# GNN kernel: GpSimd clears 960 idle numbers ahead of each batch of eight gathers in the two sum passes

## The chip, the cores and the metric

The kernel runs on one core of a Trainium2 chip. A core has TensorE (PE, matrix products; PEld is its loading of weights), VectorE (DVE), ScalarE (ACT), GpSimd (POOL), SyncE (SP) and 16 DMA engines; each engine works through its own queue in order, and the queues meet at semaphores. A gather that picks rows of a table by an index is issued by POOL. The metric is the device time of one execution in microseconds (us), as the median of several runs.

## The reference

The program is four graph networks in a row on 6250 nodes and 100000 edges (`src`, `dst`), each added to x and normalized. The change touches the fourth, whose two graph convolutions sum messages over edges:

```python
def gcn_conv(x, src, dst, W, b, n):
    h = x @ W
    loop = jnp.arange(n, dtype=src.dtype)
    s = jnp.concatenate([src, loop])
    d = jnp.concatenate([dst, loop])
    deg = jax.ops.segment_sum(jnp.ones(s.shape, h.dtype), d, num_segments=n)
    dinv = jnp.where(deg > 0, jax.lax.rsqrt(jnp.maximum(deg, 1.0)), 0.0)
    norm = dinv[s] * dinv[d]
    msg = h[s] * norm[:, None]
    out = jax.ops.segment_sum(msg, d, num_segments=n)
    return out + b
...
x = gcn_conv(x, src, dst, W1, b1, n)          # 256 -> 128
x = jax.nn.relu(batch_norm(x, g1, be1))
feats.append(x)
x = gcn_conv(x, src, dst, W2, b2, n)          # 128 -> 64
x = jax.nn.relu(batch_norm(x, g2, be2))
feats.append(x)
return jax.nn.relu(jnp.concatenate(feats, axis=1) @ Wfc + bfc)
```

The factor `dinv` of the source is put into the table's rows ahead of a pass and that of the target is applied behind it, so that the passes themselves are plain sums of table rows.

## The kernel before

The edges are sorted once by target into 832 groups (`NSLOT`) of 128 edges, such that a group's targets lie in one window of 128 nodes. For each group `order.row` has the 128 table rows to fetch, `order.place` the place of each target in its window, and `order.window` the window's number. Eight groups are a batch; there are 104 batches (`NBT`).

Stages follow one another with a barrier of all engines between them: sorting and ranking, then a1e, a2e, be and te (attention passes over the same edges, with dense stages between), then g1l (dense), the sum pass g1e on rows of 128 numbers, g2l, the sum pass g2e on rows of 64 numbers, n2 and the last product. A sum pass is `sum_pass`, written out in full for all 104 batches, with one queue for each engine:

- POOL (L1459 to L1471) issues eight gathers a batch (L1466), each of 128 rows into `rows`, a ring of four batches, that is 32 gathers. From the fifth batch on there is, ahead of the first and the fifth gather of a batch, an `apart` (L59): a wait for `s_summed` in an instruction of its own, which also counts up `s_passed`. It asks that the product that read this place of the ring is done.
- ACT builds `onehot` for a batch: eight times `distance` = |lane - place| (L1492), then relu(1 - distance) over all eight (L1495). It has two buffers.
- PE multiplies `onehot` by `rows`, one product a group (L1482; each is two matmul records in the trace), into one of eight PSUM banks. It waits for `s_onehot`, for the landing of four gathers at a time (`s_rows`), and for the bank (`s_added`).
- DVE adds the bank to the window's sums in `acc` (L1510); the window's number comes from a register that is loaded for four batches at once (L888).

No engine but POOL works for the fetching, and SP has nothing in these passes. Y is a large buffer of all stages; from g1 on it is split in `T1` and `T2` (L2321), 6400 numbers a partition each. `T1` gets the first convolution's output in g2l, `T2` the second's in n2; in both sum passes nobody reads or writes `T2`. In te, whose queue on POOL the prediction also reads, POOL has in each batch one product of its own (L1019) among the gathers (L1031), with `apart` waits on DVE's L1239.

Of the kernel before, what the change touches and what calls it, by code (L numbers as in the profile page):

```python
# [39 lines left out]
def wait(eng, sem, count):  # L40

    if isinstance(count, int) and count <= 0:
        return
    eng.wait_ge(sem, count)
# [14 lines left out]
def apart(eng, sem, count, passed):  # L59

    wait(eng, sem, count)
    eng.sem_inc(passed, 1)
# [1370 lines left out]
                batches(dve, step, NBT + 2, windows)  # L1433


def sum_pass(nc, c, stage, order, table, width, acc):

    RING = 4  # L1440
    with ExitStack() as stack:
        m = Memory(nc, stack, stage)
        rows = m.sb("rows", [P, RING, 8, width])
        onehot = [m.sb(f"onehot{b}", [P, 8, P]) for b in range(2)]
        distance = m.sb("distance", [P, 8, P], F16)
        ps_u = [m.ps(f"ps_u{b}", [P, 512]) for b in range(8)]
        s_rows = [[m.sem(f"rows{r}_{h}") for h in range(2)] for r in range(RING)]
        s_onehot, s_summed, s_added, s_distance, s_passed = (m.sem(x) for x in ("onehot", "summed", "added", "distance", "passed"))

        def lives(t):  # L1450
            return not isinstance(t, int) or 0 <= t < NBT

        def batches(eng, step, last=NBT, windows=None):
            for t in range(last):
                if windows is not None and t % RING == 0:
                    windows.load(t)
                step(t, t % RING)

        with nc.Block() as block:  # L1459
            @block.gpsimd  # L1460
            def _(pool):
                def gather(t, r):
                    for k in range(8):
                        if k % 4 == 0 and (not isinstance(t, int) or t >= RING):
                            apart(pool, s_summed, t * 8 + (k + 4 - RING * 8), s_passed)
                        pool.indirect_dma_start(  # L1466
                            out=rows[:, r, k, :], out_offset=None, in_=table,
                            in_offset=bass.IndirectOffsetOnAxis(ap=order.row[:, t * 8 + k:t * 8 + k + 1], axis=0),
                        ).then_inc(s_rows[r][k // 4], 16)

                batches(pool, gather)  # L1471

            @block.tensor
            def _(pe):
                def step(t, r):
                    b = r % 2
                    pe.wait_ge(s_onehot, t + 1)
                    for k in range(8):
                        if k % 4 == 0:
                            pe.wait_ge(s_rows[r][k // 4], t * 16 + (64 - r * 16))  # L1480
                        wait(pe, s_added, t * 8 + (k - 7))
                        pe.matmul(ps_u[k][:, 0:width], onehot[b][:, k, :], rows[:, r, k, :], start=True, stop=True).then_inc(s_summed, 1)  # L1482

                batches(pe, step)

            @block.scalar
            def _(act):
                def mark(t, b):
                    if lives(t):
                        wait(act, s_onehot, t)  # L1490
                        for k in range(8):
                            act.activation(distance[:, k, :], c.lane[:, :], ACT.Abs, scale=-1.0, bias=order.place[:, t * 8 + k:t * 8 + k + 1]).then_inc(s_distance, 1)  # L1492
                        act.wait_ge(s_distance, t * 8 + 8)
                        wait(act, s_summed, t * 8 - 8)
                        act.activation(onehot[b][:, :, :], distance[:, :, :], ACT.Relu, scale=-1.0, bias=1.0).then_inc(s_onehot, 1)  # L1495

                for t in range(NBT):
                    mark(t, t % 2)

            @block.vector  # L1500
            def _(dve):
                windows = Windows(nc, order, mybir.EngineType.DVE, -8, RING)

                def step(t, r):
                    for k in range(8):
                        if lives(t - 1):
                            mine = acc[:, bass.ds(windows.at(r, k - 8) * width, width)]
                            dve.wait_ge(s_summed, t * 8 + (k - 7))
                            wait(dve, s_added, t * 8 + (k - 8))
                            dve.tensor_tensor(mine, mine, ps_u[k][:, 0:width], ALU.add).then_inc(s_added, 1)  # L1510

                batches(dve, step, NBT + 1, windows)
# [546 lines left out]
def gnn_kernel(nc, x, src, dst,  # L2059
# [4 lines left out]
    tables = {n: nc.dram_tensor(f"table_{n}", [NPAD, n], F32, kind="Internal").ap() for n in (264, 66, 258, 256, 512, 128, 64)}  # L2064

    with ExitStack() as stack:
        m = Memory(nc, stack, "all")
        c = Keep()
        constants(nc, m, c)

        order = Keep()
# [11 lines left out]
        acc = m.sb("acc", [P, NW * 264])  # L2083
# [109 lines left out]
        with ExitStack() as st:  # L2193
# [24 lines left out]
            def drain_a2(act, ps, w, tile):  # L2218
# [6 lines left out]
                table=tables[66], table_width=66, through=ACT.Relu))  # L2225
# [12 lines left out]
        with ExitStack() as st:  # L2238
# [23 lines left out]
            def drain_ab(act, ps, w, tile):  # L2262
# [5 lines left out]
                 for h, a in enumerate((b_a1, b_a2)) for k in range(2)], x3, prepare, after_prepare=with_bias, fold=fold_attention,  # L2268
# [3 lines left out]
                            table=tables[258], table_width=258))  # L2272
# [3 lines left out]
        with ExitStack() as st:  # L2276
# [31 lines left out]
            def drain_vt(dve, ps, w, tile):  # L2308
# [8 lines left out]
                table=tables[512], table_width=512))  # L2317
# [3 lines left out]
        T1, T2 = Y[:, 0:NPAD], Y[:, NPAD:2 * NPAD]  # L2321
        dinv_of = small[:, 1, :]

        with ExitStack() as st:
# [17 lines left out]
            def drain_v(dve, ps, w, tile):  # L2342
# [5 lines left out]
                        first=Step(sources=[(y3, 0, P), (y3, P, P)], weights=[W1[:, 0, :], W1[:, 1, :]], width=256),  # L2348
                        second=Step(sources=[(x3, 0, P), (x3, P, P)], weights=[W[:, 0, :], W[:, 1, :]], width=128, drain_v=drain_v,
                                    table=tables[128], table_width=128))  # L2350
        sum_pass(nc, c, "g1e", order, tables[128], 128, acc)
        turned_norm(nc, c, "g2l", 128, acc, dinv_of, T1, (g_b1, g_g1, g_be1), g_w2, tables[64], 64)
        sum_pass(nc, c, "g2e", order, tables[64], 64, acc)
        turned_norm(nc, c, "n2", 64, acc, dinv_of, T2, (g_b2, g_g2, g_be2), ones_row=True)
        with ExitStack() as st:
            mm = Memory(nc, st, "gf")
# [37 lines left out]
```

## Time and profile before

| | us |
|---|---|
| median of 3 runs | 9835.41 |
| lowest, highest | 9833.75, 9841.89 |
| span of the profiled execution | 11006.2 |
| POOL busy in the profile | 6558.0 (60%) |
| DVE busy | 6265.2 (57%) |
| PE busy | 6188.8 (56%) |
| ACT busy | 4406.9 (40%) |

The span is from the first to the last instruction of the execution that the profiler recorded. It is the only time known of that execution, and it is 1170.8 us longer than the median of the runs without a profile. "Issue" as the releaser of an idle time means that the trace shows nothing that the engine waited for. Releasers are inferred from semaphores, and in late stages the trace sometimes names a transfer of a stage that is long over.

### The profile page before, as it was taken

The numbers are of one execution on the slowest core, as the hardware profiler recorded it, in microseconds if no ns is written. First come the engines' busy times: TensorE is split into PE (matmuls) and PEld (weight loads), VectorE is DVE, ScalarE is ACT, GpSimd is POOL, SyncE is SP. The second block draws the span as 40 slices with busy tenths as digits, with TensorE's granted clock in tenths as the row PEclk, the third lists the DMA queues.
The fourth block names the chain that finished last, engine by engine and source line by source line (L and its number), as shares of the span: only waits on it lengthen the run. The fifth ranks groups of instructions, "written<-read, shape, count | busy, mean of one in ns | idle before, by whom it ended". The sixth has DMA issues, their size and how long they took to land. (4 is left out here: it accounts for less than half of the span.)

```text
span 11006.2 us, 145249 instructions
## 1 busy us (share of the span) xinstructions
PE 6188.8 (56%) x34036; PEld 4327.9 (39%) x34036; DVE 6265.2 (57%) x19166; ACT 4406.9 (40%) x12341; POOL 6558.0 (60%) x6616
## 2 busy tenths in 40 slices
PE   3774577566666444446455557778775343433335
PEld 2443344333343444444233334445554232333334
DVE  7998899566666433335455557999984121211113
ACT  7886788222222222223222223444443233333333
POOL 4996699355554455552566642666655666566663
PEclk6997799766666555556667779999987555555556
DMA  0222122233333212212333343666652111211112
GB/s 21 74 74 67 45 73 73 87 98 99 96 98 82 62 41 41 42 41 45 105 106 107 108 93 123 175 175 175 174 159 64 46 47 45 41 27 23 23 23 35
DMA packets 464040, 862.04 MB, mean 78 GB/s; under 512 B 143184, under 2 KB 204036, under 8 KB 463108
## 3 DMA queue, kind: packets, MB, share of 16 engines
q0 software_dynamic: 226304, 550.69, 20.8%
q1 hardware_dynamic: 236932, 302.17, 9.4%
q8 instruction: 316, 5.18, 0.2%
q14 instruction: 488, 4.00, 0.1%
HBM read 800.28 MB, written 52.14 MB: 77 GB/s over the span
## 5 line engine op out<-in xcount | busy, mean ns | idle before, releaser
L1031 POOL DMA_INDIRECT all_Y<-table,all_row x3328 | 3236.2, 972 | 2394.2 <-DVE all_Y L1239 1243.1
L557 POOL TENSOR_SCALAR all_acc<-all_Y,all_acc 128x128 f16<-128x128 f16 x1176 | 1319.0, 1133 | 229.3 <-DVE all_acc L492 158.9
L1239 DVE TENSOR_TENSOR all_Y<-all_Y 128x512 f32<-128x512 f32 (+1 forms) x1560 | 942.5, 604 | 187.3 <-issue 100.3
L1466 POOL DMA_INDIRECT g2e_rows<-table,all_row x832 | 784.9, 943 | 432.3 <-issue 234.7
L1466 POOL DMA_INDIRECT g1e_rows<-table,all_row x832 | 785.1, 944 | 419.4 <-issue 234.3
L1077 PE MATMUL be_ps_u<-all_Y,be_onehot 128*128 128x258 f32 x1664 | 645.7, 523 | 546.5 <-DVE all_acc L1251 281.8
L1482 PE MATMUL g1e_ps_u<-g1e_rows,g1e_onehot 128*128 128x128 f32 x1664 | 470.3, 426 | 737.0 <-issue 557.9
L1482 PE MATMUL g2e_ps_u<-g2e_rows,g2e_onehot 128*128 128x64 f32 x1664 | 434.8, 431 | 771.9 <-issue 549.5
L1510 DVE TENSOR_TENSOR all_acc<-all_acc,g1e_ps_u 128x128 f32 x832 | 240.0, 288 | 968.0 <-DMA te_place_row<-places_src 594.5
L1077 PE MATMUL a1e_ps_u<-all_Y,a1e_onehot 128*128 128x264 f32 x1664 | 762.3, 589 | 20.1 <-DVE all_acc L1251 11.1
L1510 DVE TENSOR_TENSOR all_acc<-all_acc,g2e_ps_u 128x64 f32 x832 | 184.5, 222 | 1026.1 <-DMA te_place_row<-places_src 624.0
L1482 PEld LDWEIGHTS g2e_ps_u<-g2e_rows,g2e_onehot 128*128 128x128 f32 x1664 | 382.0, 321 | 824.8 <-issue 632.5
L1251 DVE TENSOR_TENSOR all_acc<-all_acc,be_ps_u 128x258 f32 x832 | 350.5, 421 | 606.2 <-remote 385.7
L1482 PEld LDWEIGHTS g1e_ps_u<-g1e_rows,g1e_onehot 128*128 128x128 f32 x1664 | 359.5, 275 | 847.8 <-issue 679.8
L1077 PEld LDWEIGHTS be_ps_u<-all_Y,be_onehot 128*128 128x128 f32 x1664 | 370.7, 253 | 768.5 <-issue 675.4
L495 DVE TENSOR_SCALAR all_acc<-all_Y,all_acc 128x832 f16<-128x832 f16 x1568 | 599.5, 442 | 0.0
L1063 PE MATMUL te_ps_q<-all_X,te_turned 128*128 x1664 | 515.3, 440 | 146.8 <-issue 103.6
L1077 PE MATMUL te_ps_u<-all_Y,te_onehot 128*128 128x264 f32 x1664 | 532.2, 435 | 73.6 <-DVE all_Y L1239 71.5
L1077 PE MATMUL a2e_ps_u<-all_Y,a2e_onehot 128*128 128x66 f32 x1664 | 492.1, 434 | 124.9 <-issue 86.9
L524 ACT ACTIVATE all_Y<-all_Y 128x128 f16<-128x128 f16 x1568 | 476.7, 388 | 96.4 <-PEq L81 96.4
L532 ACT ACTIVATE all_Y<-all_Y,all_acc 128x128 f16<-128x128 f16 x1568 | 477.1, 389 | 3.0 <-DMA all_Y<-codes 3.0
L1077 PEld LDWEIGHTS a2e_ps_u<-all_Y,a2e_onehot 128*128 128x128 f32 x1664 | 397.8, 318 | 145.8 <-issue 121.5
(521 smaller groups left out, 15166.9 us busy)
## 6 DMA issues: line engine op xcount, KB each, us to landing
all_Y<-table,all_row POOLq DMA_INDIRECT x3328
all_Y<-lows SPq DMA_DIRECT2D x196, 256.0 KB
all_Y<-codes SPq DMA_DIRECT2D x196, 256.0 KB
a1e_place_row<-places_dst SPq DMA_DIRECT2D x104, 256.0 KB
a2e_place_row<-places_dst SPq DMA_DIRECT2D x104, 256.0 KB
be_place_row<-places_src SPq DMA_DIRECT2D x104, 256.0 KB
te_place_row<-places_src SPq DMA_DIRECT2D x104, 256.0 KB
te_flags<-flags_src SPq DMA_DIRECT2D x832, 6.0 KB
```

The costliest lines, as they stand in the source:

```text
L495: dve.tensor_scalar(column1[b][:, k, :], lane16, column[b][:, k:k + 1], None, ALU.is_equal).then_inc(s_hot, 1)
L524: act.activation(away[:, k, :], lane16[:, 0:P], ACT.Abs, scale=-1.0, bias=low_t[:, u * 8 + k:u * 8 + k + 1]).then_inc(s_away, 1)
L532: act.activation(unlike[b][:, k, :], code_row[b][:, k * P:(k + 1) * P], ACT.Abs, scale=-1024.0, bias=spaced_t[:, u * 8 + k:u * 8 + k + 1]) ...
L557: pool.tensor_scalar(row1[b][:, k, :], lane16[:, 0:P], row[b][:, k:k + 1], other_t[:, t * 8 + k:t * 8 + k + 1], ALU.is_equal, ALU.mult).th ...
L1031: pool.indirect_dma_start(out=rows[:, r, k, :], out_offset=None, in_=table, in_offset=bass.IndirectOffsetOnAxis(ap=order.row[:, t * 8 + k: ...
L1063: last = pe.matmul(ps_q[pair % 2][:, j * HC:(j + 1) * HC], turned[b][:, k * P:(k + 1) * P], queries[:, bass.ds(windows.at(windows_j, chunk ...
L1077: pe.matmul(ps_u[k % 4][:, 0:R], onehot[b][:, k, :], summand[:, b, k, :], start=True, stop=True).then_inc(s_summed, 1)
L1239: dve.tensor_tensor(out[:, :, :, 0:C], rows[:, r, ks, value_c0:value_c0 + HC].rearrange("p k (h n) -> p k h n", h=H), bc(out[:, :, :, C:C ...
L1251: dve.tensor_tensor(mine, mine, ps_u[k % 4][:, 0:R], ALU.add).then_inc(s_added, 1)
L1466: pool.indirect_dma_start(out=rows[:, r, k, :], out_offset=None, in_=table, in_offset=bass.IndirectOffsetOnAxis(ap=order.row[:, t * 8 + k: ...
L1482: pe.matmul(ps_u[k][:, 0:width], onehot[b][:, k, :], rows[:, r, k, :], start=True, stop=True).then_inc(s_summed, 1)
L1510: dve.tensor_tensor(mine, mine, ps_u[k][:, 0:width], ALU.add).then_inc(s_added, 1)
```

## The change

`sum_pass` gets one more argument, `spare`, and both calls pass `T2`. Ahead of the first gather of each of the 104 batches POOL sets 960 float numbers of `spare` on each partition to zero and waits until that has landed (`s_rested`). Nobody reads these zeros.

```diff
-def sum_pass(nc, c, stage, order, table, width, acc):
+def sum_pass(nc, c, stage, order, table, width, acc, spare):
...
-        s_onehot, s_summed, s_added, s_distance, s_passed = (m.sem(x) for x in ("onehot", "summed", "added", "distance", "passed"))
+        s_onehot, s_summed, s_added, s_distance, s_passed, s_rested = (m.sem(x) for x in ("onehot", "summed", "added", "distance", "passed", "rested"))
...
                 def gather(t, r):
+                    pool.memset(spare[:, 0:960], 0.0).then_inc(s_rested, 1)
+                    pool.wait_ge(s_rested, t + 1)
                     for k in range(8):
                         if k % 4 == 0 and (not isinstance(t, int) or t >= RING):
                             apart(pool, s_summed, t * 8 + (k + 4 - RING * 8), s_passed)
...
-        sum_pass(nc, c, "g1e", order, tables[128], 128, acc)
+        sum_pass(nc, c, "g1e", order, tables[128], 128, acc, T2)
...
-        sum_pass(nc, c, "g2e", order, tables[64], 64, acc)
+        sum_pass(nc, c, "g2e", order, tables[64], 64, acc, T2)
```

POOL's queue at the start of g1e, before. The semaphores have the names of an earlier stage's use of the same number: `raw_src_made` is `s_summed` here.

```order
3838 L1460 UNCONDITIONAL_BRANCH [waits barrier_Pool_Activation_PE_DVE_SP_gather]
3839 L1466 DMA g1e_rows<-table,all_row 128x128 x32
3840 L1466 DMA g1e_rows<-table,all_row 128x128 [waits raw_src_made]
3841 L1466 DMA g1e_rows<-table,all_row 128x128 x3
3842 L1466 DMA g1e_rows<-table,all_row 128x128 [waits raw_src_made]
3843 L1466 DMA g1e_rows<-table,all_row 128x128 x3
```

The first 32 gathers wait for nothing, and then every fourth waits for products.

The same queue after the change, from the end of the third batch of g1e to the sixth; `count_src_prefix` is `s_rested`.

```order
3847 L1468 DMA g1e_rows<-table,all_row 128x128 x7
3848 L1463 MEMSET all_Y 128x960
3849 L1468 DMA g1e_rows<-table,all_row 128x128 [waits count_src_prefix]
3850 L1468 DMA g1e_rows<-table,all_row 128x128 x7
3851 L1463 MEMSET all_Y 128x960
3852 L1468 DMA g1e_rows<-table,all_row 128x128 [waits count_src_prefix,raw_src_made]
3853 L1468 DMA g1e_rows<-table,all_row 128x128 x3
3854 L1468 DMA g1e_rows<-table,all_row 128x128 [waits raw_src_made]
3855 L1468 DMA g1e_rows<-table,all_row 128x128 x3
3856 L1463 MEMSET all_Y 128x960
```

A memset stands ahead of every eight gathers, and the gather behind it waits for the memset. From the fifth batch on both waits are in one instruction, that of the `apart`, ahead of the gather. The other engines' queues are as they were.

## Rows read from the trace of the kernel before

**Rows 1.** The page: the span of the profiled execution.
```profile
span 11006.2 us, 145249 instructions
```

**Rows 2.** The page, groups: xcount | busy us, mean ns | idle before, releasers.
```profile
L1466 POOL DMA_INDIRECT g2e_rows<-table,all_row x832 | 784.9, 943 | 432.3 <-issue 234.7
L1466 POOL DMA_INDIRECT g1e_rows<-table,all_row x832 | 785.1, 944 | 419.4 <-issue 234.3
...
L1482 PE MATMUL g1e_ps_u<-g1e_rows,g1e_onehot 128*128 128x128 f32 x1664 | 470.3, 426 | 737.0 <-issue 557.9
...
L1510 DVE TENSOR_TENSOR all_acc<-all_acc,g1e_ps_u 128x128 f32 x832 | 240.0, 288 | 968.0 <-DMA te_place_row<-places_src 594.5
```

**Rows 3.** Gathers of both passes: ns min/median/max, first and last start.
```profile
L1466 POOL DMA_INDIRECT g1e_rows<-table,all_row x832: 938/944/1045, 8406.6 to 9597.6; - x167
L1466 POOL DMA_INDIRECT g2e_rows<-table,all_row x832: 938/944/992, 9656.9 to 10845.9; - x167
```

**Rows 4.** POOL in order of time, g1e: start, us, instruction [idle before].
```profile
9019.49 0.94 POOL L1466 DMA_INDIRECT g1e_rows<-table,all_row  x1 [0.30 <-issue]
9020.74 0.94 POOL L1466 DMA_INDIRECT g1e_rows<-table,all_row  x1 [0.30 <-issue]
```

**Rows 5.** The same view, POOL at two of its pauses in g1e.
```profile
8464.77 0.94 POOL L1466 DMA_INDIRECT g1e_rows<-table,all_row  x1 [3.48 <-DMA te_place_row<-places_src]
...
8583.83 0.94 POOL L1466 DMA_INDIRECT g1e_rows<-table,all_row  x1 [4.82 <-DMA te_place_row<-places_src]
```

**Rows 6.** Windows from the first gather: busy us (x instructions) by engine.
```profile
8406.00:8463.00 57.00, 13.38 (x46) 10.54 (x46) 4.32 (x15) 12.86 (x35) 41.63 (x44) 0.50 0.20 51
8406.00:8579.00 173.00, 58.25 (x204) 46.31 (x204) 27.10 (x94) 47.87 (x125) 117.09 (x124) 0.55 0.18 47
...
9656.00:10645.00 989.00, 351.80 (x1338) 307.67 (x1338) 146.54 (x661) 296.50 (x764) 652.85 (x692) 0.50 0.12 23
```

**Rows 7.** Instructions in order of time, ACT in g1e.
```profile
9008.65 2.44 ACT L1492 ACTIVATE g1e_distance<-all_lane,all_place 128x128 f16<-128x128 f32 x8
...
9011.13 1.06 ACT L1495 ACTIVATE g1e_onehot<-g1e_distance 128x1024 f32<-128x1024 f16 x1
```

**Rows 8.** Who waited for whom, g1e: us in total, times, longest.
```profile
DVE all_acc L1510 <- DMA te_place_row<-places_src: 592.1, 152, 6.0
```

**Rows 9.** POOL by line and form: busy us, mean ns.
```profile
L203 POOL MEMSET all_Y<- 128x896 int32 x2 | 1.7, 844 | 30.6 <-POOLq L81 30.1 <-POOLq L110 0.5
...
L214 POOL MEMSET all_X<- 128x512 f32 x1 | 0.5, 524 | 0.1
L208 POOL MEMSET all_Y<- 128x128 f16 x2 | 0.4, 204 | 0.1
```

**Rows 10.** Instructions in order of time, POOL and DVE in te.
```profile
7407.25 0.95 POOL L1031 DMA_INDIRECT all_Y<-table,all_row  x1 [0.30 <-issue]
...
7408.22 1.08 POOL L1019 TENSOR_TENSOR all_Y<-all_Y 128x512 f32<-128x512 f32 x1
...
7410.16 0.68 DVE L1239 TENSOR_TENSOR all_Y<-all_Y 128x512 f32<-128x512 f32 x1
...
7411.63 0.98 POOL L1031 DMA_INDIRECT all_Y<-table,all_row  x1 [2.33 <-DVE all_Y L1239]
```

**Rows 11.** Instructions in order of time, POOL at the start of the kernel.
```profile
4.86 0.84 POOL L203 MEMSET all_Y<- 128x896 int32 x1 [0.48 <-POOLq L110]
5.64 0.84 POOL L204 MEMSET all_Y<- 128x896 int32 x1
6.44 0.82 POOL L206 IOTA all_acc<- 128x832 int32 x1
...
8.26 0.20 POOL L208 MEMSET all_Y<- 128x128 f16 x1
8.54 0.29 POOL L209 TENSOR_SCALAR_AFFINE_SELECT all_Y<-all_ones 128x128 f32<-128x128 f32 x1
```

## The prediction

> **What bounds the kernel now.** I read the page's groups of instructions first, then the two sum passes by line, then POOL's order in time. The profiled execution spans 11006.2 us [rows 1]; the timed runs have a median of 9835.41, 1170.8 less. A sum made in the profile may therefore hold stalls that the timed runs do not have, and I keep that apart from the start.
>
> The change touches only the passes g1e and g2e. In each, 832 gathers are issued by POOL, at 944 and 943 ns, with 419.4 and 432.3 us of idle time between them [rows 2]. From the first gather of a pass to its last it is 9597.6 - 8406.6 = 1191.0 us in g1e and 10845.9 - 9656.9 = 1189.0 in g2e [rows 3]. For most of a pass POOL goes at one fixed pace: a gather starts 1.25 us after the one before (9019.49, 9020.74), 0.94 of work and 0.30 of idle [rows 4]. 831 such steps are 1039 us. The rest, 152 us in g1e and 150 in g2e, is a few dozen pauses of some microseconds, two of which are shown: 3.48 us of idle before 8464.77 and 4.82 before 8583.83 [rows 5].
>
> Does another engine make POOL pause? A gather waits only for a place in the ring of 32: before gather i (counted from 0, at every fourth) POOL wants i + 4 - 32 products done. Up to 8463 POOL has issued 44 gathers and PE has 46 matmul records, two to a product, so 23 products; gather 44 needs 16. Up to 8579 it is 124 gathers and 102 products, and gather 124 needs 96. Up to 10645 in g2e it is 692 gathers and 669 products against 664 [rows 6]. So the products that POOL needs are there when it pauses; a release by the transfer of te_place_row, of an earlier stage, is no true releaser [rows 5]. The other engines are far from their limit. In a batch of eight, POOL's pace gives 8 x 1.25 = 10.0 us. ACT needs 2.44 + 1.06 = 3.5 us [rows 7], DVE's adds take 8 x 0.29 of work, and PE is busy 470.3/104 = 4.5 us a batch [rows 2]. DVE does have long waits for nothing that can be its releaser, 592.1 us in 152 times [rows 8], but its delay does not reach POOL through the ring by the counts above. **POOL's own queue sets the length of both passes**, and there is nothing beside it that would hide work added to that queue.
>
> **The change, part by part.** The two passes have 104 batches each, so 208 memsets of 960 numbers on each of 128 partitions, 208 waits for them, and no work taken away.
>
> *The memset.* POOL's memsets of other sizes give its duration: 204 ns for 128 numbers, 524 for 512, 844 for 896 [rows 9]. That is 97 ns and 0.833 ns a number, so 97 + 960 x 0.833 = **0.90 us**. The type doesn't move it as far as the rows show: 128 numbers of two bytes lie on the same line as 512 and 896 of four.
>
> *Getting into it.* In te a POOL tensor operation follows a gather: the gather ends at 7407.25 + 0.95 = 8.20 and the operation starts at 8.22 [rows 10]. So **0.02 us**, and the 0.30 that stands between two gathers belongs to the start of a gather and comes again after the memset.
>
> *Getting out of it.* This is the term that decides. Without the wait POOL's sequencer prepares a gather while the one before is under way, which is why only 0.30 shows. With the wait it stands until the memset has landed, and then has the wait's instruction and a whole gather to prepare. The trace of before has no wait of POOL on POOL before a gather. The nearest row is te's wait on DVE, with the same instruction (a wait with an increment) and then a gather: DVE's L1239 ends at 7410.16 + 0.68 = 10.84 and the gather starts at 11.63, **0.79 us** [rows 10]. The lower end is 0.36: the 0.30 of any gather and 0.06 for a POOL operation that waits for POOL (the linked memset of 128 ends at 8.26 + 0.20 = 8.46 and its follower starts at 8.54, 0.08) [rows 11]. I take 0.79, since that row has the same two instructions.
>
> *Sum.* A batch gains 0.02 + 0.90 + 0.79 and keeps out the 0.30 that it had there: **1.41 us**. 208 x 1.41 = **293 us**. With the low end it is 0.02 + 0.90 + 0.36 - 0.30 = 0.98, and 204 us. With no credit for the 0.30 it is 1.71, and 356, which I hold for too much because the 0.30 is in te's 0.79 too. In the ring's terms nothing turns: behind the waiting instruction stand eight gathers, behind them PE's products and DVE's adds, which all move back by the same 1.41 a batch and have 5 us of slack in it. The first memset of a pass delays the first gather by as much as any other. The ends of the passes don't change.
>
> Memset and adds could meet in SBUF. The gathers run beside the adds all the time and their median is 944 ns with a minimum of 938 [rows 3], and the 844 ns of the memset of 896 [rows 9] were taken with no add beside them. Nothing shows a price for two of them together, so I put nothing, and the range has room for it.
>
> The Trainium skill (Perfetto Trace Analysis, GPSIMD Engine Instruction) says that reported durations of GpSimd instructions are not to be trusted and that the distance from start to start should be used. The rows bear on it: the memsets of 896 follow each other at 4.86, 5.64 and 6.44, which is 0.79 apart and not 0.84 [rows 11]. By that rule the new memset costs 0.85, a batch 1.36, and the sum would be 283 us instead of 293; that does not change which case is likeliest.
>
> Against the profile's own time the sum is 11006.2 + 293 = 11299. The timed runs are 1170.8 us shorter than the profile. Of that the pauses of the sum passes can be 302 at most, and if they are gone in a timed run, POOL's pace alone sets the pass, which is where an addition counts in full. So I carry the 293 over unchanged: 9835.4 + 293 = **10128 us**, 3.0% more.
>
> **Rivals.**
>
> *The wake-up is short* (POOL waking POOL is quicker than DVE waking POOL). For: the linked operations of [rows 11] have 0.08 between them. Against: they are no gathers. 0.98 to 1.25 a batch gives +204 to +260, 10039 to 10095.
>
> *The pauses soak it up.* If POOL's pauses exist in timed runs and come from something that goes by its own clock and not by POOL's count of instructions, the rest before a batch is taken out of them. 302 us of pauses stand against 293 of memsets: the time would be 9835 to 9850, the same. For: DVE and POOL show waits at the same time with false releasers [rows 5, 8]. Against: the timed runs lack 1170.8 us that must come from stalls of this kind. If half of the pauses are there, +150, 9985.
>
> *The rest pays* (the case on the other side). What makes POOL pause may be a backlog that builds up in some 24 to 30 gathers and is worked off while POOL is still. A rest ahead of every eight gathers could keep it from building. Its place is the start of a gather's wait, its price for a pass is 104 rests, its gain at most the 151 us of pauses. It wins if a rest costs less than 151/104 = 1.45 us and all pauses go. With 0.98 a rest that is 102 - 151 = -49 a pass, -98 in all, 9737. At 1.41 it is -8 for both passes, no difference. It needs the pauses in the timed runs, all of them prevented and the short wake-up at once.
>
> *The change doesn't do what it says*: the memset could be hidden beside the gathers if POOL didn't wait. The order has the wait on the instruction right behind each memset in both passes, so I give it nothing of its own.
>
> **How the numbers follow.** The forecast, 1.25 to 1.55 a batch with no cover, has 0.60. The short wake-up has 0.20. Half covered, from +50 to +200, 0.09. Soaked up, 0.07. The rest pays, 0.03, and 0.01 for more than +325. The range goes from 9990, which takes in the short wake-up and the upper part of the half covered cases, to 10160, 1.56 a batch; it leaves out about 0.15. About 0.2%, 20 us, is what a measurement of this kernel can tell from no change. Faster by more than that: 0.03; within it: 0.07; slower: 0.90.
>
> **What would show it.** In the profile of the changed kernel: 104 memsets in each pass at 0.85 to 0.90 us; after each, 0.79 us of idle before the gather (0.36 if the wake-up is short); gathers still 0.94 long and 1.25 apart inside a batch; from first to last gather 1191 + 103 x 1.41 = 1336 us a pass if the pauses stay, 1184 + pauses if they shrink. PE's and DVE's busy time must be what it was. I am wrong if the passes keep their 1190 us with fewer pauses (soaked up), or if a gather behind the memset starts much later than 0.8 us. The step that I trust least is that what POOL pauses for in the profile has no part in the timed runs.

## The result: 3.1% slower on one chip, and no difference on another

| | us |
|---|---|
| median before (4 runs, 9832.33 to 9841.89) | 9834.58 |
| median after (4 runs, 10133.27 to 10143.3) | 10138.29 |
| ratio, 95% interval | 1.0306 (1.0293 to 1.0318) |
| span of the profiled execution after | 10139.6 |

The change costs 303.7 us; forecast were 293. One thing has to be known to read any number here: the chips differ. On some the median of the kernel before is 9824 to 9835 us, on others 11018 to 11115, with no run in between, and the profile that the prediction was read from (11006.2 us [rows 1]) is of the second kind while the times were of the first. Each experiment below is compared with runs of before on its own chip, which I call a quick chip or a chip with pauses. Each chip was used on one occasion only, so the runs cannot tell the chip from the occasion.

The two sum passes hold only 302 of the 1170.8 us between that profile and the times. The first gather of g1e starts at 8406.6 in [rows 3] and at 7535.9 in the profile of the change (below): 870.7 us more lie ahead of the passes, where the two kernels are the same. By the first instruction of each stage, a1e is some 350 us longer than on a quick chip, a2e 320 and be 205, and te is as long as there.

The page after, its span and the groups that answer to [rows 2] (line 1466 is now 1468, 1482 is 1484, 1510 is 1512):

```profile
span 10139.6 us, 145457 instructions
...
L1468 POOL DMA_INDIRECT g2e_rows<-table,all_row x832 | 785.7, 944 | 316.5 <-issue 210.5
L1468 POOL DMA_INDIRECT g1e_rows<-table,all_row x832 | 785.7, 944 | 316.5 <-issue 209.3
L1484 PE MATMUL g1e_ps_u<-g1e_rows,g1e_onehot 128*128 128x128 f32 x1664 | 428.7, 439 | 784.2 <-issue 468.2
...
L1512 DVE TENSOR_TENSOR all_acc<-all_acc,g1e_ps_u 128x128 f32 x832 | 240.2, 289 | 971.9 <-PE g1e_ps_u L1484 841.1
```

The gathers are 944 ns as before, and DVE's idle time, which had false releasers in [rows 2], now ends with PE's products: DVE simply waits for data. The two passes by line, as [rows 3], and the memsets (ns min/median/max, first and last start):

```profile
L1468 POOL DMA_INDIRECT g1e_rows<-table,all_row x832: 940/944/1045, 7535.9 to 8730.9; - x167
L1468 POOL DMA_INDIRECT g2e_rows<-table,all_row x832: 940/944/992, 8790.3 to 9985.3; - x167
```

```profile
L1463 POOL MEMSET all_Y<- x208: 897/917/923, 7534.7 to 9974.9; 128x960 f32 x104
```

Both passes go from first to last gather in 1195.0 us. POOL in order of time, in the middle of g1e:

```profile
8003.64 0.94 POOL L1468 DMA_INDIRECT g1e_rows<-table,all_row  x1 [0.30 <-issue]
8004.57 0.92 POOL L1463 MEMSET all_Y<- 128x960 f32 x1
8006.30 0.95 POOL L1468 DMA_INDIRECT g1e_rows<-table,all_row  x1 [0.81 <-POOL all_Y L1463]
8007.56 0.94 POOL L1468 DMA_INDIRECT g1e_rows<-table,all_row  x1 [0.30 <-PE g1e_ps_u L1484]
```

The memset starts at the gather's end, takes 0.92, and 0.81 of idle time follows it. From gather to gather across it are 2.66 us and not 1.25: 1.41 to 1.42 a batch. In the first four batches of a pass it is less, because there is no ring wait yet and the gather itself carries the wait for the memset; the idle time is 0.27 and the step across the memset 2.13, which is 0.88 more than 1.25:

```profile
7544.72 0.94 POOL L1468 DMA_INDIRECT g1e_rows<-table,all_row  x1 [0.30 <-issue]
7545.66 0.92 POOL L1463 MEMSET all_Y<- 128x960 f32 x1
7546.85 0.95 POOL L1468 DMA_INDIRECT g1e_rows<-table,all_row  x1 [0.27 <-POOL all_Y L1463]
```

### The profile page after: what moved, and what is told of

Read it like the earlier page. It is cut to its first block and busy times, and to the rows that moved or that the text cites. A ratio compares the mean times of both kernels' runs of the same rounds, so it can differ in the third digit from the quotient of the medians.

```text
span 10139.6 us, 145457 instructions
## 1 busy us (share of the span) xinstructions
PE 6119.0 (60%) x34036; PEld 4326.3 (43%) x34036; DVE 6273.3 (62%) x19166; ACT 4403.1 (43%) x12341; POOL 6786.5 (67%) x6824
## 5 line engine op out<-in xcount | busy, mean ns | idle before, releaser
L1031 POOL DMA_INDIRECT all_Y<-table,all_row x3328 | 3275.0, 984 | 1490.4 <-issue 1043.1
L1484 PE MATMUL g1e_ps_u<-g1e_rows,g1e_onehot 128*128 128x128 f32 x1664 | 428.7, 439 | 784.2 <-issue 468.2
L1484 PE MATMUL g2e_ps_u<-g2e_rows,g2e_onehot 128*128 128x64 f32 x1664 | 406.5, 426 | 805.7 <-issue 477.3
L1077 PE MATMUL be_ps_u<-all_Y,be_onehot 128*128 128x258 f32 x1664 | 670.9, 563 | 297.1 <-DVE all_acc L1251 296.8
L1077 PE MATMUL a1e_ps_u<-all_Y,a1e_onehot 128*128 128x264 f32 x1664 | 729.2, 565 | 26.6 <-DVE all_acc L1251 24.6
L1077 PEld LDWEIGHTS be_ps_u<-all_Y,be_onehot 128*128 128x128 f32 x1664 | 411.4, 275 | 516.4 <-issue 396.9
L1497 ACT ACTIVATE g2e_onehot<-g2e_distance 128x1024 f32<-128x1024 f16 x104 | 109.8, 1056 | 815.3 <-PE g2e_ps_u L1484 815.2
```

What stands on the lines that cost most here:

```text
L1031: pool.indirect_dma_start(out=rows[:, r, k, :], out_offset=None, in_=table, in_offset=bass.IndirectOffsetOnAxis(ap=order.row[:, t * 8 + k: ...
L1077: pe.matmul(ps_u[k % 4][:, 0:R], onehot[b][:, k, :], summand[:, b, k, :], start=True, stop=True).then_inc(s_summed, 1)
```

## The experiments

The runs were made on four chips, two with pauses and two quick ones.

### The kernel before, profiled again

> The kernel before, unchanged, for a second profile. Theory (POOL's own queue sets both sum passes; the pauses in the first profile of before are of that one profiled execution): the profiled span is near 9833, the gathers of g1e and g2e go from first to last in 1040 to 1055 us each, with no pause above 2 us but a few, and the change then adds about 145 us to each. Rival (the pauses belong to the kernel, and the memset's rest prevents them): the passes are again 1190 us with some 40 pauses of 3 to 6 us, and the timed difference of 304 us cannot be found in them.

On a chip with pauses: 11120.7 us against 11115.5, ratio 1.0006 (0.9995 to 1.0017). The pauses are there again. Its gathers and its span:

```profile
span 11110.0 us, 145249 instructions
```

```profile
L1466 POOL DMA_INDIRECT g1e_rows<-table,all_row x832: 938/944/1045, 8483.2 to 9682.7; - x167
L1466 POOL DMA_INDIRECT g2e_rows<-table,all_row x832: 938/944/992, 9750.3 to 10953.6; - x167
```

```profile
8543.77 0.94 POOL L1466 DMA_INDIRECT g1e_rows<-table,all_row  x1 [5.86 <-DMA te_place_row<-places_src]
8545.01 0.94 POOL L1466 DMA_INDIRECT g1e_rows<-table,all_row  x1 [0.30 <-issue]
```

So pauses like those of [rows 5] are not a freak of one execution, as the theory had it; they come with such a chip. This profile is of one of the timed executions (11111.8 us), so they are in its timed runs too. The passes take 1199.5 and 1203.3 us there. The expectation of 1040 to 1055 failed on this chip. It is met on a quick chip (the kernel of fewer updates, below).

### The memset without a stall

```diff
-                    pool.memset(spare[:, 0:960], 0.0).then_inc(s_rested, 1)
-                    pool.wait_ge(s_rested, t + 1)
+                    if t > 0:
+                        pool.wait_ge(s_rested, t)
+                    pool.memset(spare[:, 0:960], 0.0).then_inc(s_rested, 1)
```

> The same memset of 960 ahead of each batch, but POOL waits for the memset of the batch before, done some 10 us earlier, so nothing stalls. Theory: the memset's 0.92 us counts in full and the wake-up is gone: 0.92 a batch, +191 us against before (of the 304 of the change). Rival (the memset runs beside the descriptor work of the gathers and only the wait costs): 0 to +40 us.

On a chip with pauses: 1.0000 (0.9988 to 1.0012). By the time alone neither theory could be told there. The order of time can: at the start of the pass, ahead of any pause, the memset is not beside the gather but behind it.

```profile
8485.40 0.94 POOL L1469 DMA_INDIRECT g1e_rows<-table,all_row  x1 [0.30 <-issue]
8486.34 0.91 POOL L1465 MEMSET all_Y<- 128x960 f32 x1
8487.42 0.95 POOL L1469 DMA_INDIRECT g1e_rows<-table,all_row  x1 [0.16 <-issue]
```

From gather to gather 2.02 us, so 0.77 more and not 0.92, since only 0.16 of idle time follows; 2.02 is the median step across all the memsets of both passes too. The rival (hidden work) is out as far as POOL's order goes; what the 0.77 would be in a timed run of a quick chip was not measured.

### The change with 2 numbers in place of 960

> The change with 2 numbers in place of 960, same wait. Theory: the memset falls to 0.12 us, the idle time behind it stays 0.81: 0.02 + 0.12 + 0.81 - 0.30 = 0.62 to 0.65 a batch in 200 batches and 0.1 in the 8 first ones, +125 to +131 us against before. Rival (only the memset's length counts): +20 us; rival (the idle time behind the memset is its own draining and shrinks with it): +20 to +60 us.

On a chip with pauses: 1.0004 (0.9994 to 1.0014), nothing, where +125 was expected. It was the first sign that the added time vanishes there. On a quick chip:

> The change with 2 numbers in place of 960, on another occasion. On a chip without pauses: 0.62 to 0.65 a batch, +125 to +131 us against before. On a chip with pauses POOL's own work is 1039 + 65 us a pass, less than the 1190 of before, and the time stays within 15 us of before.

9967.2 us against 9830.0, ratio 1.0135 (1.0115 to 1.0155), +137 us with +125 to +131 expected (the interval is +113 to +152). The expectation left out nine pauses a pass, 24 us in all, that the change brings with it (last section), and passes that end some 4 us sooner behind their last gather ("The sum", below).

```profile
8002.60 0.94 POOL L1468 DMA_INDIRECT g1e_rows<-table,all_row  x1 [0.30 <-issue]
8003.54 0.12 POOL L1463 MEMSET all_Y<- 128x2 f32 x1
8004.47 0.95 POOL L1468 DMA_INDIRECT g1e_rows<-table,all_row  x1 [0.81 <-POOL all_Y L1463]
```

The idle time behind the memset is the same 0.81 for 2 numbers as for 960. So it is no draining of the memset but the price of the wait. With the 0.12 of the memset and less the 0.30 that stood there before, a batch costs 0.62, where the change costs 1.42.

### The wait carried by the gather

```diff
                     for k in range(8):
                         if k % 4 == 0 and (not isinstance(t, int) or t >= RING):
                             apart(pool, s_summed, t * 8 + (k + 4 - RING * 8), s_passed)
+                        if k == 0:
+                            pool.memset(spare[:, 0:960], 0.0).then_inc(s_rested, 1)
+                            pool.wait_ge(s_rested, t + 1)
```

(in place of the same two lines ahead of the loop)

> The change with the memset put behind the ring's wait, so that the wait for the memset is carried by the gather itself and not by a waiting instruction with an increment ahead of it. Theory (it is the separate waiting instruction that keeps the sequencer from preparing the gather; seen in the first four batches of a pass, 0.27 us of idle time instead of 0.81): 0.88 a batch in all 208, +183 us against before. Rival (a wait behind a memset costs 0.81 whichever instruction carries it): +290 to +305 us, as the change.

On a chip with pauses 1.0019 (1.0006 to 1.0032), +20 us. Again on another such chip:

> The wait for the memset carried by the gather itself, once more. On a chip without pauses: 0.88 a batch in 208, +183 us against before; rival +290 to +305. On the chip with pauses it gave +20 (1.0006 to 1.0032 as a ratio), expected again.

0.9999 (0.9988 to 1.0009): the +20 did not come back. On the first of the two chips the profile shows part of it: the passes take 1211.4 and 1207.9 us there, 16.5 more in sum than in the kernel before, profiled again; on the second they take 1191.4 and 1193.5. And on a quick chip:

> The change with the wait for the memset carried by the gather itself. On a chip without pauses: the first batches of earlier profiles have 2.13 us from gather to gather across the memset and not 2.67, so 0.88 a batch in all 208 and perhaps some 1.36 us pauses, +183 to +205 us against before, where the change has +304. Rival (the timed cost of a wait behind a memset is the same whichever instruction carries it): +290 to +305. On a chip with pauses: within 20 us of before, as twice so far.

10006.3 us against 9823.7, ratio 1.0184 (1.0167 to 1.0201): **+182.6 us, with +183 to +205 expected** and +290 to +305 for the rival. POOL in the middle of g1e, and its pass:

```profile
8044.18 0.94 POOL L1469 DMA_INDIRECT g1e_rows<-table,all_row  x1 [0.30 <-issue]
8045.12 0.92 POOL L1467 MEMSET all_Y<- 128x960 f32 x1
8046.31 0.95 POOL L1469 DMA_INDIRECT g1e_rows<-table,all_row  x1 [0.27 <-POOL all_Y L1467]
```

```profile
L1469 POOL DMA_INDIRECT g1e_rows<-table,all_row x832: 940/944/1045, 7535.1 to 8664.2; - x167
```

The same memset and the same wait cost 0.88 a batch and not 1.42 when the waiting instruction is the gather. What the change pays for beside the memset is that its wait fell into the `apart`, an instruction of its own ahead of the gather.

### The change on a chip with pauses, and twice the memset

> The change as it is, beside the kernel before on the same chip. Where the kernel before takes about 9835 us (passes without pauses), both theories expect 10138, +304. Where it takes about 11115 (the chip of the first four experiments, on which the semaphore updates of TensorE come late and POOL pauses some 160 us a pass): theory 1 (a rest on POOL is taken out of its pauses, up to what they hold, 1.55 a batch) expects 0 to +60 us, with fewer pauses and the passes at 1200 to 1215 us; theory 2 (the pauses are added to whatever POOL does) expects +290 to +300.

11016.3 us against 11017.7, ratio **1.0004 (0.9993 to 1.0014)**. The change that costs 304 us on a quick chip costs nothing here that can be told from noise. Theory 1 holds and theory 2 is out; the passes are even a little shorter than its 1200 to 1215 us. The pass in this run:

```profile
L1468 POOL DMA_INDIRECT g1e_rows<-table,all_row x832: 940/944/1045, 8399.7 to 9594.7; - x167
```

It takes 1195.0 us, to the tenth what it takes on the quick chip: with a rest of 1.42 a batch POOL waits for no product any more, and goes by its own queue alone. The pass of before on such chips takes 1189.0 to 1203.3 ([rows 3] and above), 1037 of its own and 152 to 166 of pauses. The rests and the pauses change places nearly one for one: on the chip of the first four experiments the passes take 1199.5 and 1203.3 us with no rest, 1200.8 and 1199.5 with 0.62 a batch (2 numbers), 1203.9 and 1203.3 with 0.77 (no stall), 1211.4 and 1207.9 with 0.88 (the gather waits).

```diff
-                    pool.memset(spare[:, 0:960], 0.0).then_inc(s_rested, 1)
+                    pool.memset(spare[:, 0:1920], 0.0).then_inc(s_rested, 1)
```

> The change with 1920 numbers in place of 960, same wait. On a chip without pauses: 0.80 a batch more than the change, 2.22 in 200 batches and 1.68 in 8, +457 us against before. On the chip with pauses, theory 1 (pauses soak up at most what they hold): POOL's own work is 1039 + 229 = 1268 us a pass, 65 to 70 more than the passes of before, +130 to +180 us; theory 2: +450.

11181.0 us, ratio 1.0153 (1.0136 to 1.0170), +163 us with +130 to +180 expected. There is nothing left to take the second 0.80 out of:

```profile
L1468 POOL DMA_INDIRECT g1e_rows<-table,all_row x832: 940/944/1045, 8424.4 to 9701.7; - x167
```

```profile
8702.49 1.72 POOL L1463 MEMSET all_Y<- 128x1920 f32 x1
8705.02 0.95 POOL L1468 DMA_INDIRECT g1e_rows<-table,all_row  x1 [0.81 <-PE g1e_ps_u L1484]
```

The pass is 1277.3 us, 82.3 more than with 960, which is 0.80 for each of the 103 memsets between its first gather and its last.

### The memset on VectorE

```diff
                 def step(t, r):
+                    if t < NBT:
+                        dve.memset(spare[:, 0:960], 0.0).then_inc(s_rested, 1)
+                        dve.wait_ge(s_rested, t + 1)
                     for k in range(8):
```

> The same memset and wait, but on VectorE ahead of its eight adds, POOL's queue as before. Theory (POOL's own queue sets the passes, VectorE has 5 us of slack a batch): on a chip without pauses 0, within 20 us. Rival (the passes hang on the whole loop, or the memset takes VectorE's and GpSimd's shared way to SBUF and slows the gathers): +100 to +250 us. On the chip with pauses VectorE waits for updates and not for itself: 0 to +30.

On a chip with pauses: 1.0006 (0.9995 to 1.0017), with 178.5 us of memsets on DVE.

```profile
L1506 DVE MEMSET all_Y<- 128x960 f32 x208 | 178.5, 858 | 141.7 <-issue 83.7 <-PE g2e_ps_u L1482 17.9 <-PE g1e_ps_u L1482 16.9
```

```profile
L1466 POOL DMA_INDIRECT g1e_rows<-table,all_row x832: 942/947/1046, 8424.0 to 9617.0; - x167
```

It fits, but on such a chip rests on POOL cost nothing either, so it says little of what would happen on a quick one. That was not tried.

### Fewer semaphore updates

```diff
-                        pe.matmul(ps_u[k][:, 0:width], onehot[b][:, k, :], rows[:, r, k, :], start=True, stop=True).then_inc(s_summed, 1)
+                        last = pe.matmul(ps_u[k][:, 0:width], onehot[b][:, k, :], rows[:, r, k, :], start=True, stop=True)
+                        if k % 4 == 3:
+                            last.then_inc(s_summed, 1)
...
+                            if k == 7:
+                                last.then_inc(s_distance, 1)
```

(with the waits on both counted accordingly; no memset)

> The kernel before (no memset) with fewer semaphore updates in both sum passes: PE tells of four products at a time and not of one, ACT of eight distances and not of one. Of some 155 updates a batch (128 by the gathers' 16 DMA engines, 8 by PE, 8 by DVE, 9 by ACT, 2 by POOL) 13 go. Theory A (on the chips with pauses all updates share a way of limited rate, which the passes of 1190 us go by): 1190 x 142/155 = 1090 a pass, -200 us. Theory B (only the updates of the DMA engines fill that way, or it is something else that comes with gathers): within 30 us of before. On a chip without pauses POOL's own queue sets the passes and both expect 0.

> The kernel before with 13 of some 155 semaphore updates a batch left out in the sum passes. On a chip with pauses, theory A (all updates share one way of limited rate): -200 us; theory B (it is the updates of the DMA engines, or something else that comes with gathers): within 30 us of before. On a chip without pauses 0, as before.

Both came to quick chips: 0.9998 (0.9988 to 1.0009) and 1.0003 (0.9994 to 1.0013), as both theories expect there. What delays POOL on the chips with pauses was so not settled. But the profile is that of a quick pass with no memset, which is what the first experiment was to show:

```profile
L1466 POOL DMA_INDIRECT g1e_rows<-table,all_row x832: 940/944/1045, 7528.3 to 8565.7; - x167
L1466 POOL DMA_INDIRECT g2e_rows<-table,all_row x832: 940/944/992, 8629.1 to 9666.3; - x167
```

```profile
8042.65 0.94 POOL L1466 DMA_INDIRECT g1e_rows<-table,all_row  x1 [0.30 <-issue]
8043.89 0.94 POOL L1466 DMA_INDIRECT g1e_rows<-table,all_row  x1 [0.30 <-issue]
```

1037.4 and 1037.2 us, 831 steps of 1.248 and no pause.

## Why the prediction was right

**POOL's own queue sets both passes.** Right on the quick chips, where the forecast was tested. A pass is 831 gathers at POOL's pace, 1037.4 us; with the change 1195.0; with the wait on the gather 1129.1. The times follow: +304, +183, and +137 with 2 numbers. What POOL got was paid but for a few us at the ends of the passes. On the chips with pauses this step of the prediction does not hold: there the passes go by something else, which takes in rests of up to 1.42 a batch.

**The sum.** It had 0.02 + 0.90 + 0.79 - 0.30 = 1.41 a batch. Measured are 0.00 for getting into the memset, 0.92 for it, 0.81 behind it, 1.42 in 100 batches and 0.88 in the first four. For a pass 100 x 1.42 + 3 x 0.88 (the first memset lies ahead of the first gather) is 145 us; measured are 1195.0 - 1037.4 = 157.6. Of the missing 13, 12.2 are nine pauses that the sum did not have (last section). Twice 157.6, and 1.2 for each first memset, is 318, and the time moved by 304 (288 to 313 by the interval).

"The ends of the passes don't change" was wrong, and it takes 9 us off. From the start of a pass's last gather to the end of DVE's last add it is 13.3 and 13.0 us in the profile of the change and 17.8 and 17.5 in that of the kernel of fewer updates, whose time is that of before. So the passes themselves grow by 309 us, inside the interval; the 5 us that are left are less than the 10 by which the quick chips differ in the kernel before. The forecast of 293 is as near as it is partly by luck: the pauses that it lacks (+24) stand against the shorter ends (-9) and the first batches, which cost 0.88 and not 1.41 (-4).

**The wake-up** was the term that decides, bounded by 0.36 and 0.79, and taken from te's wait on DVE because that row had the same two instructions. It was 0.81, and the two experiments on it show that both cases exist: 0.81 behind a waiting instruction of its own, and 0.27, below even the lower bound, when the gather waits. The sentence that the lower end belongs to POOL waking POOL was wrong in its reason. Who wakes whom hardly matters (0.79 behind DVE, 0.81 behind POOL), which instruction waits does. Choosing by the nearest row in kind, and not by the nearest engine, was the step that made the number.

**The unmatched profile.** The prediction said that the 1170.8 us between profile and timed runs had to be stalls of the kind of [rows 5], and carried the 293 over unchanged. The conclusion held. The reason was not that a profile adds stalls: chips with pauses run the same kernel at 11018 to 11115 us when timed. Nor did the difference in time force the pauses of the passes to be gone: they are 302 of the 1170.8, the rest is in a1e, a2e and be. The step that I trusted least was indeed the one on which all hung. That it held was luck in part: it hung on which chip was timed, and on the other kind it would have failed.

**"The products that POOL needs are there when it pauses."** By the matmul records of [rows 6] yes, and yet the pauses are true waits. In the same windows DVE had done 94 adds where PE had done 102 products: all eight banks were full, and DVE waited for news of products that were long done. In that trace the updates of `s_summed` come one in 4 to 6 us (9013.91, 9018.91, 9023.83, ... 9047.64) and then eight of them 0.04 us apart, just when POOL has been still for three microseconds. DVE's adds follow these updates and not the products: the three below start 0.14 us after those of 9028.72, 9033.62 and 9039.22 (start, us, [idle before]):

```profile
9028.86 0.29 DVE L1510 TENSOR_TENSOR all_acc<-all_acc,g1e_ps_u 128x128 f32 x1 [4.61 <-DMA te_place_row<-places_src]
9033.76 0.29 DVE L1510 TENSOR_TENSOR all_acc<-all_acc,g1e_ps_u 128x128 f32 x1 [4.61 <-DMA te_place_row<-places_src]
9039.36 0.29 DVE L1510 TENSOR_TENSOR all_acc<-all_acc,g1e_ps_u 128x128 f32 x1 [5.31 <-DMA te_place_row<-places_src]
```

POOL waits for the same semaphore. So the pauses go by late updates, which the records of the products do not show, and my counting proved less than it claimed. One reserve: on the chips with pauses the trace lacks some of these update records (678 of 832 are there in this pass, all of them on the quick chips), so it is the adds that carry this reading. A slower TensorE is not the reason, since its granted clock in the two passes of before is 0.58 and 0.50, and 0.50 in both on a quick chip.

**The rivals.** *Soaked up* had 0.07 and is what happens on the chips with pauses: 1.0004 for the change. The reasoning for its size (302 us of pauses against 293 of memsets) held as well: one memset length more and the time moves by 163. *The rest pays*: the rest does keep the pauses from building up, with 1.42 a batch all of them go, and it gives nothing, as its own working had it for that price (-8 us). With the cheaper rest of 2.02 us across the memset some pauses stay, and no time is won either: its passes take 1203.9 and 1203.3 us. A smaller rest that beats before was not found. *The wake-up is short* is true of the first four batches only.

None of the versions beats the kernel before on a chip on which it was timed.

## What to carry to other kernels

Work added to a queue that nobody holds up costs its full length, and the wait behind it can cost as much as the work: look at which instruction carries the wait, and let the expensive one carry it itself where it can (0.27 us of idle time here in place of 0.81). Compare a profile's span with the timed runs before using it; where they differ by a tenth, find out which stalls are in only one of them, and say for both cases what a change does. A stall that gives way to added work one for one can point to a limit somewhere else, and doubling the added work shows where it ends.

## What the runs showed of the hardware

**A wait in an instruction of its own ahead of a gather costs 0.54 us more than one that the gather carries.** 0.81 us from the end of a memset of 2, 960 or 1920 numbers to the gather behind a wait of its own, 0.27 us when the gather waits. It fits that a waiting instruction keeps POOL's sequencer from preparing the gather; the trace does not show the preparing itself.

**Chips differ in how soon semaphore updates are seen.** With the gathers running at 1.25 us, DVE adds a product up to eight products and 40 us after its end on some chips (in before's g1e 5.8 us in the median), and none of the 18 passes profiled on such chips took less than 1189.0 us; on the quick ones a pass takes 1037.4, and with the change an add starts 0.73 us after its product at the latest. More rest on POOL makes the delay smaller on the chips with pauses: with the change 116 of the 832 adds of g1e come over 1 us late, the worst 17.9 us, and POOL does not feel it; with twice the memset none does. What limits the rate there is open. With the change both kinds of chip take the same 1195.0 us for a pass.

**A pause of 1.36 us in every 88 gathers.** In the profile of the change the second gather of a batch starts 2.61 us after the first, at every eleventh batch:

```profile
8074.76 0.95 POOL L1468 DMA_INDIRECT g1e_rows<-table,all_row  x1 [0.81 <-POOL all_Y L1463]
8077.37 0.94 POOL L1468 DMA_INDIRECT g1e_rows<-table,all_row  x1 [1.66 <-issue]
8078.62 0.94 POOL L1468 DMA_INDIRECT g1e_rows<-table,all_row  x1 [0.30 <-issue]
```

It is there nine times a pass with 960, with 2 and with 1920 numbers, and in no quick pass without memsets. With the wait on the gather, on a quick chip, 0.05 of it is left: at the same nine places the step is 1.30. It does not need the memset either. On the chips with pauses the kernel before has it at some of the same places, each time behind a gather for which POOL had to wait. These are the first and the second gather of a batch of g1e (numbers 200 and 201, counted from 0) in its second profile, where a wait ends at the first:

```profile
8770.77 0.94 POOL L1466 DMA_INDIRECT g1e_rows<-table,all_row  x1 [1.74 <-DMA te_place_row<-places_src]
8773.38 0.94 POOL L1466 DMA_INDIRECT g1e_rows<-table,all_row  x1 [1.67 <-issue]
```

So something comes up every 88 gathers, which a queue that runs ahead hides and one that was just held up does not. What it is stays open. The fetching of code would be a guess, and two readings speak against it: the distance is 88 gathers with 110 instructions of POOL between two places (no memset) and with 121 (with it), and in 17 of the 18 pauses in the profile of the change the trace's instruction queues transfer nothing.

**The length of a memset.** The Trainium skill (Perfetto Trace Analysis, GPSIMD Engine Instruction) would have GpSimd timed from start to start. Here the memset of 960 shows as 0.91 or 0.92, and lengthens the way from gather to gather by 0.77 where nothing waits for it (in the profile of the memset without a stall): the 0.85 that the prediction worked out by that rule was nearer to it than the 0.90 of the durations. Where something waits for it, 0.92 and the idle time behind it are what counts.
